# Masking the last row of attention blocks: in the score product on TensorE instead of on VectorE

## The reference

```
x = x + attention(gn(x))        # windows of 64 tokens, 8 heads of 16, rotary positions
x = x + batch_norm_relu(conv1(gn(x)))
x = x + dense_stack(gn(x))      # twice
```

```
attn = softmax(q * scale @ k.T + mask)      # 64 x 64
out  = attn @ v
```

## Time and profile before

| | |
|---|---|
| Median of 3 runs | 2349.58 us (2347.5 to 2351.88) |
| The profiled execution | 2355.57 us |
| Its span, first to last instruction | 2353.8 us |
| PE (TensorE matmul) busy | 2040.5 us, 87% |
| DVE (VectorE) busy | 1701.4 us, 72% |
| ACT (ScalarE) busy | 1166.2 us, 50% |
| POOL (GpSimd) busy | 1070.6 us, 45% |
| Granted TensorE clock, mean | 0.954 |

### The profile page before, as it was taken

The page is one execution under the profiler, slowest core; times in us unless marked ns, Lnnn a source line. Parts: engine busy times, 40 slices in busy tenths (PEclk is TensorE's granted clock), DMA queues, the critical chain, the costliest instruction groups (busy, mean ns, idle before and its releaser), DMA issues. The chain is left out here.

```text
span 2353.8 us, 75176 instructions
## 1 busy us (share of the span) xinstructions
PE 2040.5 (87%) x30482; PEld 1082.7 (46%) x30482; DVE 1701.4 (72%) x3497; ACT 1166.2 (50%) x2603; POOL 1070.6 (45%) x1234
## 2 busy tenths in 40 slices
PE   6599979997999799985999169898999999999996
PEld 5455545554555455543655123343444443333332
DVE  4598998899898989893433578887676766555553
ACT  6577656665666566751222245453443433333330
POOL 0287767776777677765920264332222211111100
PEclk8799999999999999996999579999999999999997
DMA  8301111111111011111222677785444444444444
GB/s 233 109 25 49 36 46 36 50 36 45 37 49 36 32 50 38 47 33 50 100 98 95 250 248 222 235 241 147 140 136 125 128 135 109 122 123 124 123 101 105
DMA packets 259007, 243.82 MB, mean 104 GB/s; under 512 B 124784, under 2 KB 230512, under 8 KB 258672
## 3 DMA queue, kind: packets, MB, share of 16 engines
q1 hardware_dynamic: 258672, 239.09, 33.6%
HBM read 92.45 MB, written 89.65 MB: 77 GB/s over the span
## 5 line engine op out<-in xcount | busy, mean ns | idle before, releaser
L1226 POOL TENSOR_SCALAR l_x<-l_x,l_scale,l_shift 128x384 f32<-128x384 f32 x192 | 150.2, 782 | 594.2 <-PE banks L1644 589.4
L435 POOL TENSOR_TENSOR at_prob<-at_prob,at_inv 128x512 f32<-128x512 f32 x288 | 294.2, 1042 | 116.5 <-DVE at_inv L575 111.3
L501 ACT ACTIVATE at_prob<-at_prob 128x512 f32<-128x512 f32 x288 | 181.9, 632 | 306.9 <-DVE at_prob L565 306.8
L1602 PE MATMUL banks<-l_a,l_taps 128*32 128x384 f32 x3456 | 312.7, 493 | 19.7 <-ACT l_r L1298 19.7
L1617 PE MATMUL banks<-l_above,l_taps 128*32 128x384 f32 x1728 | 307.6, 489 | 3.3 <-issue 2.1
L1617 PE MATMUL banks<-l_below,l_taps 128*32 128x384 f32 x1728 | 306.3, 489 | 0.0
L1309 ACT ACTIVATE l_above<-l_below 96x384 f32<-96x384 f32 x144 | 75.4, 524 | 440.3 <-DVE l_below L1488 228.6
L617 PE MATMUL banks<-at_xn,at_w 128*64 128x256 f32 x2336 | 286.0, 387 | 1.8 <-ACT at_xn L453 1.4
L1474 DVE COPY l_old<-l_a 32x384 f32<-32x384 f32 x576 | 243.6, 423 | 11.4
L656 PE MATMUL banks<-const,at_prob 128*128 128x128 f32 x1152 | 184.4, 287 | 51.6 <-POOL at_prob L435 50.8
L416 POOL TENSOR_TENSOR at_turn<-at_turn,at_tables 128x256 f32<-128x256 f32 x292 | 215.3, 759 | 1.0 <-ACT at_turn L472 0.9
(11 more groups left out here) (160 smaller groups left out, 3607.4 us busy)
## 6 DMA issues: line engine op xcount, KB each, us to landing
l_x<-both SPq DMA_DIRECT2D x48, 768.0 KB, 4.7
l_rows<-l_r SPq DMA_DIRECT2D x768, 48.0 KB, 2.0
l_work<-both SPq DMA_DIRECT2D x36, 768.0 KB, 6.0
at_k_bd<-at_k SPq DMA_DIRECT2D x584, 32.0 KB, 1.8
load_raw<-in_x SPq DMA_DIRECT2D x36, 512.0 KB, 4.8
both<-c_y SPq DMA_DIRECT2D x96, 192.0 KB
both<-l_x SPq DMA_DIRECT2D x24, 768.0 KB, 4.0
out<-l_x SPq DMA_DIRECT2D x24, 768.0 KB, 4.5
```

Of the source, the lines that this page charges most:

```text
L435: nc.gpsimd.tensor_tensor(prob[i][p][:, :, :], prob[i][p][:, :, :], inv[i][p][:, :].unsqueeze(2).broadcast_to([P, HEADS, WIN]), ALU.mult). ...
L501: nc.scalar.activation(prob[j % 2][p][:, :, :], prob[j % 2][p][:, :, :], ACT.Exp).then_inc(s["exped"], 1)
L1602: last = nc.tensor.matmul(grid(acc(k)[block_rows(c), :]), e[kind_of(k)][:, dy + 1, dx, :], a[:, k % A_RING, rows_, dx:dx + SIDE], start=(d ...
```

## The change

The table with the limits is replaced by two. `T_IS` holds, in its row `c`, a 1 where the token in that column is of region `c` (rows 0 to 2 of each 64; all others are 0, since no region has their number). `T_FAR` holds -3e38 in rows 0 to 2 where the token is not of region `c`. The product of the two is -3e38 for a masked pair and 0 for an allowed one. In masked steps each score matmul leaves its accumulation open, and a second matmul adds this product into the same quarter and PSUM region, with `T_FAR` repeated for the four heads by a step of zero. The minimum on VectorE, its wait and its semaphore are gone; maximum and subtraction read PSUM in every step.

```diff
-T_CQ, T_SQ, T_CK, T_SK, T_LIM, T_END = 0, 64, 128, 192, 256, 320
+T_CQ, T_SQ, T_CK, T_SK, T_IS, T_FAR, T_END = 0, 64, 128, 192, 256, 320, 384
...
-    out[:, T_LIM:T_LIM + WIN] = np.where(region[c % WIN][:, None] == region[None], FAR, -FAR)
+    of = (c % WIN)[:, None]
+    out[:, T_IS:T_IS + WIN] = region[None] == of
+    out[:, T_FAR:T_FAR + WIN] = np.where((region[None] != of) & (of < 3), -FAR, 0.0)
...
-                    if row.masked:
-                        table = tables[:, T_LIM:T_LIM + WIN].unsqueeze(1).unsqueeze(1).broadcast_to(split)
-                        nc.vector.tensor_tensor(out, src, table, ALU.min).then_inc(s["limited"], 1)
-                        src = out
-                        dve.wait_ge(s["limited"], row.b * (2 * ROW_STEPS) + 2 * j + p + 1)
...
-            def score(n, i):
+            def score(n, i, masked):
...
-                        last = nc.tensor.matmul(
-                            ps_s[rows, half, QUAD * p:QUAD * (p + 1)].rearrange("p (h m) -> p h m", m=WIN),
-                            q_r[i][heads, WIN * wdw:WIN * (wdw + 1)],
-                            k_bd[i][heads, :, WIN * wdw:WIN * (wdw + 1)], start=True, stop=True)
+                        out = ps_s[rows, half, QUAD * p:QUAD * (p + 1)].rearrange("p (h m) -> p h m", m=WIN)
+                        last = nc.tensor.matmul(out, q_r[i][heads, WIN * wdw:WIN * (wdw + 1)],
+                                                k_bd[i][heads, :, WIN * wdw:WIN * (wdw + 1)], start=True,
+                                                stop=not masked)
+                        if masked:
+                            far = tables[heads, T_FAR:T_FAR + WIN].unsqueeze(1).broadcast_to([WIN, HEADS // 2, WIN])
+                            last = nc.tensor.matmul(out, tables[heads, T_IS:T_IS + WIN], far, start=False, stop=True)
                 last.then_inc(s["scores"], 1)
...
-                score(n, j % 2)
+                score(n, j % 2, row.masked)
```

More of the change, by code:

```diff
@@ L338, in attention_stage @@
             "qk", "k_turned", "q_kept", "q_turned",
-            "q_r", "k_r", "v_bd", "scores", "limited", "top", "shifted", "exped", "summed", "inv",
+            "q_r", "k_r", "v_bd", "scores", "top", "shifted", "exped", "summed", "inv",
             "normed", "turned", "copied", "pv", "o_buf", "projected", "added",
```

## The result

The changed kernel takes 2332.12 us (median of 4 runs, 2328.03 to 2333.48) against 2348.54 before (4 runs): ratio 0.992, 95% interval 0.991 to 0.994. A second comparison, on another chip, gave 0.992 again (0.991 to 0.993). It is faster by 0.8%, where 0.75% was forecast.

What follows compares the result with a forecast made beforehand. VectorE, 96% busy, bounds masked rows. The mask's 35.0 us come back, less 17.2 for longer scores and 0.1 for the table: net -17.7, so 2331.9 us. Range 2327 to 2337, with rival 2 up to 2353.

Steps and rivals of the forecast that it cites:

- the ring: Attention step from scores through VectorE, ScalarE's copies and TensorE's weighing to the next scores: 6.61 us, no engine full.
- the growth of the scores: Masked step: mask matmuls lengthen the scores by 0.86 us, from 1.09 to 1.95, paid in five of six steps.
- rival 1: Masked rows: the mask matmuls are free, all 35.0 us come back, 2314.6 us; chance 0.03.
- the first step's slack: First step of a row: VectorE is late, scores wait 1.03 us for it, so the 0.86 growth is hidden there.
- four more in a row cost 0.86: Each quarter gets 8 records in a row instead of 4, at 0.215 us each, priced from the input projection.
- the forecast of 17.7: Whole kernel: net gain in us, 35.0 given back less 17.2 for score growth and 0.1 for the table.
- The subtraction's price: Masked step on VectorE: two subtractions reading PSUM (0.691 us) instead of SBUF (0.948) save 0.257 us each.
- Rival 3: Masked scores: pairs in one quarter serialise, scores about 4.1 us, 3.0 more, time 2382 us; chance 0.17.
- my reason for 0.70: Chance 0.70 for 0.86 us growth, because overlap follows the number of tiles: quarters 5.7 deep, sixteenths 17 deep.
- Rival 2: Mask matmuls cost about twice their peers, scores grow 1.2 to 2.1 us, time 2339.2 to 2352.0; chance 0.10.
- Its turning point, 1.63 us: Score growth at which six steps' growth less 1.03 us of slack equals the mask's 8.76 us, ending the gain.
- The table's longer load: Start of the attention stage: 32 KB more on a 160 KB load, under 0.7 us once, taken as 0.1.

Runs made afterwards that it cites:

- bf16 mask: Changed kernel with both mask tables cast once to bf16, program order unchanged: 2327.41 us, ratio 0.989 to the kernel before.
- bf16 mask twice: Changed kernel with each mask matmul in bf16 and done twice with half the value, behind its score matmul: 2330.76 us, run once.
- mask in rounds: Changed kernel with, in each half of a masked step, four score matmuls first, then four mask matmuls, one per quarter: 2336.04 us, ratio 0.993.
- twice, in rounds: Changed kernel with each mask matmul done twice at half value, in rounds of four scores, four masks, four masks per half: 2355.05 us, ratio 1.000.
- bf16 mask three times: Changed kernel with each mask matmul in bf16 and done three times with a third of the value, behind its score matmul: 2359.13 us, run once.
- quarter by quarter: Changed kernel with all four matmuls of a quarter (two scores, two masks) behind each other in masked steps, then the next quarter's: 2398.77 us, ratio 1.019.
- twice, in place: Changed kernel with each mask matmul done twice with half the value, directly behind its score matmul: 2409.66 us, ratio 1.024.

## Why the prediction was right, and where it was lucky

- **What bounds a masked row.** VectorE before the change, the ring after it: shown by the row without the mask (38.48, like an ordinary row) and by the growth of the scores against the length of the row. The row without the mask answers rival 1 as well: the mask's matmuls are not free, they cost 4.01 us an image. With growth g of the scores the prediction's account gives 38.48 + 5g up to g = 1.03 (the first step's slack), and 38.48 + 6g - 1.03 beyond:

| kernel | g, us | row by the account | row measured |
|---|---|---|---|
| bf16 mask | 0.23 | 39.6 | 39.52 |
| bf16 mask twice | 0.50 | 41.0 | 40.87 |
| mask in rounds | 0.87 | 42.8 | 42.63 |
| the change | 0.93 | 43.1 | 43.00 |
| twice, in rounds | 1.73 | 47.8 | 47.61 |
| bf16 mask three times | 1.79 | 48.2 | 47.78 |
| quarter by quarter | 3.61 | 59.1 | 58.69 |
| twice, in place | 3.83 | 60.4 | 60.05 |

The rows come out 0.1 to 0.4 us shorter than the account.

- **The growth of the scores.** 0.86 was forecast, 0.93 came; in rounds it is 0.87. The step "four more in a row cost 0.86" holds.
- **The first step** hides the growth, as said (2.19 to the maximum, as before).
- **A term that I missed:** the step behind a masked row gives back 0.51 us. In the last masked step VectorE no longer idles before it turns k (0.45 us in the last ordinary step of the kernel before, none in the first line below), so it comes to the next row less late: the first maximum there follows 1.68 us after the scores' start at 334.38, and not 2.19.

```profile
332.55 0.86 DVE L545 SCALAR_TENSOR_TENSOR at_turn<-banks,at_bias,at_tables 128x256 f32<-128x256 f32 x2
...
336.06 0.65 DVE L559 TENSOR_REDUCE at_top<-banks 128x8 f32<-128x512 f32 x1
```

  That is 2.0 us of gain. With 0.9 us lost, since the masked row took 43.00 us and not 42.78, the forecast of 17.7 became 19.0 by the rows (17.7 + 2.0 - 0.9, and 0.1 that the table did not cost).
- **Where luck helped.** The medians fell by 16.4 us, with an interval of 15 to 22, which holds both 17.7 and 19.0. That the time forecast, 2331.9, lies 0.2 from the 2332.12 measured is luck: the two errors above, 2.0 and 0.9, partly cancel, and the four runs of each kernel spread over more than 5 us. And the change stays within the limit on records with nothing to spare: with one record more in a pair the gain was gone.
- **The subtraction's price** was read from a mean. The prediction puts 0.257 us on each of the two subtractions of a step; it is 0.51 on the first and nothing on the second, and goes with GpSimd's work, as shown above. The sum of a step is the same, and the forecast did not rest on it, as it took the mask's cost from the starts of the scores.
- **Rival 3, the serialised pairs,** is false for the change but its mechanism is real. I argued that TensorE, which passes one blocked record of each quarter, would pass three. It does, and three is the limit. With five records in a row the scores take 2.88 us, where the sum without a limit gave 1.75, and nothing is left of the gain (a masked row of 47.78 us against 47.02). No row before the change showed this limit, and my reason for 0.70 (overlap in proportion to the tiles) did not bear on it: that the pair stayed within it was luck.
- **Rival 2,** a mask at half rate, is false: the repeated operand streams like any other (1.96 us in rounds). Its turning point, 1.63 us, was a little low. With the 0.51 us that the step behind gives back it is (8.76 + 0.51 + 1.03) / 6 = 1.72, and 1.73 measured 1.000, where the prediction had 2.4 us of loss.
- **The Trainium skill's rule of strict order** is refuted more plainly than I could before. The program alternates score and mask matmul for each quarter, but in the masked step at 305.52 all eight score records of a half start before the first mask record at 306.00. TensorE does not keep the program's order between quarters; in every run the starts fit an order that is kept within one. The Trainium skill's page TensorE: Matmul & The Clock Gate (section The mechanism) has matmuls start strictly in program order; the measurement decides here.
- **The table's longer load** left no trace: it landed in 2.9 us, against 3.5 before.

## What to carry to other kernels

Price an edit in the stage's ring, from scores to the next scores, and not in the busy time of the engine that it relieves: VectorE lost 10 us of work in a masked row, the row 4. Where TensorE works in tiles, deal matmuls to them in turn, and count records (two for fp32, one for bf16) before putting several of one tile together. Where GpSimd works at the same time, let VectorE's two-operand instructions read one operand from PSUM if the data lie there anyway.

## What the runs showed of the hardware

- A quarter (64 x 64) of the array takes four records, one running and three waiting; with the fifth, everything behind it stands still until one has started (scores 1.59 us with four in a row, 2.88 with five; 4.92 with six and 4.70 with eight, of fp32). This is read from the starts: the next quarter's first record came within 0.01 us of the moment when three of the quarter's records were left to start, with five, six and eight in a row.
- An fp32 matmul of 256 columns leaves two records that start 0.216 us apart; a bf16 one leaves one, and two of them in a quarter lengthened the scores by 0.23 us.
- The same subtraction takes 0.691 us when it reads the scores from PSUM, with GpSimd at work or not. From SBUF it takes 0.691 with GpSimd all but idle, and 1.21 in the mean with GpSimd at work. That GpSimd's work causes the loss was not tried by itself.
